# Layer 0 on a fixed SBUF map, layer 1's first loads issued inside layer 0, and its weights turned in six banks

## What is computed

```python
x = L0_attn_x                                  # [2, 1024, 512]
xn = _layernorm(x)
s = _L0_attn_ref(xn, Wq, bq, Wk, bk, Wv, bv)   # attention over the 16 dims of a head, per token
g = _silu(_L0_ffn_ref(xn, gate_w, ...))        # top 2 of 3 experts, chosen per batch entry
x = x + s * g
xn = _layernorm(x)
s = _L1_attn_ref(xn, Wq, Wk, Wv, Wo)           # causal attention with rotary positions, 32 heads, 8 key/value heads
g = _silu(_L1_ffn_ref(xn, qweight_gu, ...))    # gated FFN with 4-bit weights, unpacked in the kernel
x = x + s * g
```

## Time and profile before

| what | us |
|---|---|
| runs: median of three | 1476.67 |
| runs: lowest, highest | 1471.11, 1478.86 |
| the profiled execution's own time | 1469.95 |
| its span, from first to last instruction | 1468.2 |
| PE busy in the span | 1337.5 (91%) |
| DVE busy | 1058.9 (72%) |
| ACT busy | 618.0 (42%) |
| POOL busy | 334.9 (23%) |

### The profile page before, as it was taken

How to read it: one execution, slowest core, us unless ns; L and a number is a source line. 1 busy time by engine, 2 the same in 40 slices (tenths; PEclk the granted TensorE clock), 3 DMA queues, 4 the chain that set the end, 5 groups by cost and what they waited for, 6 DMA issues and landing times.

```text
span 1468.2 us, 19974 instructions
## 1 busy us (share of the span) xinstructions
PE 1337.5 (91%) x6642; PEld 924.9 (63%) x6642; DVE 1058.9 (72%) x2495; ACT 618.0 (42%) x859; POOL 334.9 (23%) x387
## 2 busy tenths in 40 slices
PE   3788988992998899999999998999999999999998
PEld 2557676772765677777777764555555555555467
DVE  6887978684787555555555476888888888888557
ACT  4633755452442111111111111666666666666662
POOL 2653667361332000000000000222112222212221
PEclk9978998995999899999999995999999999999999
DMA  6101200005344100000000050111122132231002
GB/s 213 63 24 63 72 16 29 0 29 184 96 124 135 53 27 27 25 22 22 22 13 12 5 97 0 34 34 34 34 44 56 34 90 62 63 68 29 2 29 86
DMA packets 45165, 76.11 MB, mean 52 GB/s; under 512 B 9556, under 2 KB 16804, under 8 KB 45076
## 3 DMA queue, kind: packets, MB, share of 16 engines
q1 hardware_dynamic: 43086, 73.36, 18.1%
q10 hardware_dynamic: 1990, 1.62, 0.4%
HBM read 55.67 MB, written 19.01 MB: 51 GB/s over the span
## 4 chain that ended last, share of the span: by engine, by line
PE 63%; DVE 6%; ACT 2%; issue 2%; DVEq 1%; ACTq 1%; DMA 0%; POOL 0%; SPq 0%; POOLq 0%
PE d_bank L1835 12%; PE d_bank L37 10%; PE d_bank L1875 10%; PE d_bank L1859 9%; PE d_bank L39 9%; PE d_bank L38 9%; PE d_bank L1883 1%; DVE mx_first L1595 1%; DVEq L1598 1%; DVE hl L1451 1%; DVE d_bank L1592 1%; PE d_bank L1704 1%; DVE hs L1448 1%; PE d_bank L1814 1%; ACT hh L1350 1%
## 5 line engine op out<-in xcount | busy, mean ns | idle before, releaser
L1386 ACT ACTIVATE prob<-d_bank 128x1024 f32<-128x1024 f32 (+3 forms) x384 | 302.3, 811 | 212.8 <-PE d_bank L1859 209.2
L1592 DVE CUSTOM_DVE_ANT_0 d_bank<-d_bank,mask 128x128 f32<-128x128 f32 (+3 forms) x512 | 246.2, 504 | 43.4 <-PE d_bank L1835 35.8
L1835 PE MATMUL d_bank<-kst,qst 96*128 96x512 f32 (+3 forms) x768 | 264.4, 386 | 5.4 <-DVE mx_first L1595 3.2
L1835 PEld LDWEIGHTS d_bank<-kst,qst 96*128 96x128 f32 x768 | 145.4, 194 | 145.1 <-DVE mx L1592 51.7
L1859 PE MATMUL d_bank<-qst,kst 98*128 98x512 f32 (+3 forms) x768 | 210.7, 357 | 0.5 <-ACT prob L1386 0.5
L1251 POOL TENSOR_SCALAR_AFFINE_SELECT prob<-prob 128x256 f32<-128x256 f32 x256 | 103.9, 406 | 449.9 <-ACT prob L1386 448.4
L1595 DVE TENSOR_REDUCE mx_first<-d_bank 128x1 f32<-128x512 f32 x256 | 176.3, 689 | 27.0 <-PE d_bank L1835 19.7
L1875 PE MATMUL d_bank<-prob,vst 128*32 128x512 f32 (+3 forms) x1536 | 164.5, 500 | 1.1 <-POOL prob L1251 1.1
L1342 ACT ACTIVATE hs<-d_bank 128x512 f32<-128x512 f32 (+1 forms) x44 | 26.3, 598 | 304.1 <-PE d_bank L39 304.1
L37 PE MATMUL d_bank<-xtl,wgh 128*128 (+1 forms) x352 | 141.3, 402 | 11.0 <-DVE v_all L1537 11.0
L1859 PEld LDWEIGHTS d_bank<-qst,kst 98*128 98x128 f32 x768 | 130.0, 192 | 19.0 <-ACT prob L1386 8.2
(11 more groups left out here) (256 smaller groups left out, 2419.1 us busy)
## 6 DMA issues: line engine op xcount, KB each, us to landing
wst<-L_ffn_w SPq DMA_DIRECT2D x8, 1024.0 KB, 6.9
qst<-q_scr SPq DMA_DIRECT2D x32, 256.0 KB, 4.8
qw<-L_ffn_qweight_gu SPq DMA_DIRECT2D x40, 128.0 KB, 2.6
xb<-L_attn_x SPq DMA_DIRECT2D x4, 1024.0 KB, 6.7
x_d<-xb SPq DMA_DIRECT2D x4, 1024.0 KB, 4.3
xb<-x_d SPq DMA_DIRECT2D x4, 1024.0 KB, 6.7
q_scr<-qh SPq DMA_DIRECT2D x16, 256.0 KB
q_scr<-ql SPq DMA_DIRECT2D x16, 256.0 KB
```

The source lines that it names most:

```text
L1386: act.activation(prob[:, c // 2 % 2, c % 2 * 2:c % 2 * 2 + 2, lo:], score_bank[c % 2][:, :, lo:], ACT.Exp, scale=D ** -0.5).then_inc(exp_d ...
L1592: dve.tensor_tensor_reduce(sc, sc, mask[:, CH - w:CH], 1.0, LEAST, ALU.add, ALU.max, mx[:, u, h % 2, h // 2, q:q + 1]).then_inc(spare_free, 1)
L1835: pe.matmul(spare_bank(number)[:, 0:w], qst[u][0:M_ROW, h // 2, q * P:q * P + P], kst[u][0:M_ROW, h % 2, at:at + w], start=True, stop=True ...
```

## The change

`layer0` gets a map of SBUF with fixed places; a class `Shared` holds what both layers use: the identity, the buffer of layer 1's tokens, the buffer of its weights, and three semaphores. The buffers' bytes overlap layer 0's staging buffers 0, 1 and 2, but no other tensor of layer 0. The last chunk's input and output (`xb[0]`) lie apart from all that layer 1 writes at first.

```diff
+class Shared:
+    def __init__(self, nc, ctx):
+        self.ident = place(nc, "ident", [P, P], F32, 203.5)
+        self.xb = place(nc, "xb1", [P, 2, TPC, E], F32, 0)
+        self.wqkv = place(nc, "wqkv", [P, QKT // P, E], F32, 123.5)
+        self.x1_stored, self.x_in, self.w_in = (ctx.enter_context(nc.semaphore("d_" + n)) for n in ("x1_stored", "xin0", "w_in"))
...
# layer0, SP: after the store of chunk c
+                if c == 2:
+                    sp.wait_ge(w1_ready, SL * B)
+                    sp.dma_start(shared.xb[:, 0], x1v[:, 0]).then_inc(shared.x_in, 16)
+                    sp.wait_ge(w2_ready, SL * B)
+                    Wq1, Wk1, Wv1 = next_qkv
+                    sp.dma_start(shared.wqkv[:, 0:KT], Wq1.rearrange("(o p) e -> p o e", p=P)).then_inc(shared.w_in, 16)
+                    sp.dma_start(shared.wqkv[:, KT], Wk1).then_inc(shared.w_in, 16)
+                    sp.dma_start(shared.wqkv[:, KT + 1], Wv1).then_inc(shared.w_in, 16)
-            sp.wait_ge(xout[0], 32)
             sp.wait_ge(xout[1], 16)
             sp.wait_ge(xout[2], 16)
...
# layer1, SP
-            sp.dma_start(xb[:, 0], x1v[:, 0]).then_inc(xin[0], 16)
-            sp.dma_start(wqkv[:, 0:KT], Wq.rearrange("(o p) e -> p o e", p=P)).then_inc(w_in, 16)
-            sp.dma_start(wqkv[:, KT], Wk).then_inc(w_in, 16)
-            sp.dma_start(wqkv[:, KT + 1], Wv).then_inc(w_in, 16)
             sp.dma_start(xb[:, 1], x1v[:, 1]).then_inc(xin[1], 16)
+            sp.dma_start(rotate[:, :], rotate_d).then_inc(rotate_in, 16)
+            sp.dma_start(cos[:, :], cos_d).then_inc(table_in, 16)
+            sp.dma_start(sin[:, :], sin_d).then_inc(table_in, 16)
+            small = lambda to, a: sp.dma_start(to, a).then_inc(s_in, 16)
+            small(sg[:, :], flat_gu(sc_gu, P))
...
             quants(0, 0, *PIECES[0])
             quants(0, 0, *PIECES[1])
+            sp.wait_ge(shared.x1_stored, 32)
             reload(2)
             keep_small_arrays()
+            sp.dma_start(mask[:, :], mask_d).then_inc(const_in, 16)
+            sp.dma_start(fixed[:, :, :], fixed_d).then_inc(const_in, 16)
...
# layer1, ACT: all fifteen loads leave its stream; the weights' parts come ahead of the tokens
-            normalize(0, range(TPC))
             for o in range(OT):
                 act.wait_ge(w_tp, o + 1)
-                act.activation(wth[:, :, o * P:o * P + P], bank[:, 2 + o % 2].rearrange("p (k q) -> p k q", k=KT),
+                act.activation(wth[:, :, o * P:o * P + P], bank[:, 2 + o].rearrange("p (k q) -> p k q", k=KT),
                                ACT.Copy).then_inc(w_hi, 1)
+            normalize(0, range(TPC))
             high_parts(0, range(TPC))
...
# layer1, PE
             pe.wait_ge(w_in, 48)
-            pe.wait_ge(ident_in, 16)
-            pe.wait_ge(const_in, 48)
             for o in range(OT):
-                if o >= 2:
-                    pe.wait_ge(w_lo, o - 1)
                 for k in range(KT):
-                    mm = pe.transpose(bank[:, 2 + o % 2, k * P:k * P + P], wqkv[:, o, k * P:k * P + P], ident[:, :])
+                    mm = pe.transpose(bank[:, 2 + o, k * P:k * P + P], wqkv[:, o, k * P:k * P + P], ident[:, :])
...
             turn_tokens(0, range(TPC))
             pe.wait_ge(w_lo, OT)
+            pe.wait_ge(rotate_in, 16)
```

More of the change, by code:

```diff
@@ L39, in three, with place, layer0 @@
     return pe.matmul(out, wh, mh, start=False, stop=last)
-def layer0(nc, x, Wq, bq, Wk, bk, Wv, bv, gate_w, gate_b, w1, b1, w2, b2, ident_d, strength_d, x1_d):
+def place(nc, name, shape, dt, at):
+    return nc.alloc_sbuf_tensor_at(name, shape, dt, offset=BASE + int(at * 1024))
+class Shared:
[4 more added lines that the diff above has]
+        self.x1_stored, self.x_in, self.w_in = (ctx.enter_context(nc.semaphore("d_" + n)) for n in ("x1_stored", "xin0", "w_in"))
+def layer0(nc, shared, x, Wq, bq, Wk, bk, Wv, bv, gate_w, gate_b, w1, b1, w2, b2, ident_d, strength_d, x1_d, next_qkv):
     with ExitStack() as ctx:
+        free = [[8, 123.5], [139.5, 171.5], [179.5, 203.5], [204, 207.75]]
         def sb(name, shape, dt=F32):
-            return ctx.enter_context(nc.sbuf_tensor(name, shape, dt))
+            size = math.ceil(math.prod(shape[1:]) / 8) / 32
+            room = next(r for r in free if r[1] - r[0] >= size)
+            room[0] += size
+            return place(nc, name, shape, dt, room[0] - size)
         def sem(name):
@@ L109, in layer0 @@
         x3_in = sem("x3_in")
-        xout = [sem(f"xout{u}") for u in range(UB)]
+        xout = [shared.x1_stored] + [sem(f"xout{u}") for u in range(1, UB)]
         w_in = [sem(f"w_in{u}") for u in range(WB)]
@@ L321, in high_part_w @@
                     act.wait_ge((f1_ps, f2_step)[n % 2], last)
[L322 removed]
+                act.activation((w1h, w2h)[n % 2][:, s], wst[n % WB][:, :, :], ACT.Copy).then_inc(hi_done, 1)
             def functions(c, m):
@@ new lines, in layer1 @@
+        cos, sin = place(nc, "cos", [P, T], F32, 16), place(nc, "sin", [P, T], F32, 20)
+        qf, qc = place(nc, "qf", [P, 2, CH], F32, 24), place(nc, "qc", [P, 2, CH], F32, 28)
+        wth, wtl = place(nc, "wth", [P, KT, QKT], F32R, 147.5), place(nc, "wtl", [P, KT, QKT], F32R, 159.5)
+        qh, ql = place(nc, "qh", [P, HALVES, CH], F32R, 189), place(nc, "ql", [P, HALVES, CH], F32R, 195)
+        rotate = place(nc, "rotate", [P, P], F32, 201)
+        stats, mv = place(nc, "stats1", [P, TPC, 6], F32, 201.5), place(nc, "mv1", [P, TPC, 2], F32, 201.625)
@@ L923, in layer1 @@
-        hot = place("hot", [2 * SD, 3, P], F32R, 187.5)
-        hs = place("hs", [P, 2, CH], F32, 189)
-        hh, hl = place("hh", [P, 2, CH], F32R, 193), place("hl", [P, 2, CH], F32R, 197)
-        ident, mask = place("ident", [P, P], F32, 203.5), place("mask", [P, CH], F32, 204)
-        mt = place("mt", [HG * QB, STACKS, P], F32R, 206)
-        fixed = place("fixed", [P, 2, 1], F32, 207.5)
-        qst = [place(f"qst{u}", [P, 2, T], F32R, at) for u, at in enumerate((112, 128, 171.5))]
-        kst = [place(f"kst{u}", [P, 2, T], F32R, at) for u, at in enumerate((120, 136, 179.5))]
@@ new lines, in layer1 @@
+        hh, hl = place(nc, "hh", [P, 2, CH], F32R, 193), place(nc, "hl", [P, 2, CH], F32R, 197)
+        mask = place(nc, "mask", [P, CH], F32, 204)
+        mt = place(nc, "mt", [HG * QB, STACKS, P], F32R, 206)
+        fixed = place(nc, "fixed", [P, 2, 1], F32, 207.5)
+        qst = [place(nc, f"qst{u}", [P, 2, T], F32R, at) for u, at in enumerate((112, 128, 171.5))]
+        kst = [place(nc, f"kst{u}", [P, 2, T], F32R, at) for u, at in enumerate((120, 136, 179.5))]
+        vst = place(nc, "vst", [P, STACKS, QB, 2 * D], F32, 144)
```

186 lines of the change are left out of this document (86 added, 100 removed).

## The result

The changed kernel took 1461.84 us (median of 10 runs, 1454.64 to 1464.27), the kernel before 1474.18 us in runs on the same chip (10 runs, 1469.97 to 1478.86). The ratio is 0.9906, its 95% interval 0.9884 to 0.9928: faster by 12.3 us, 0.9%. The forecast was 1460.5 in 1453 to 1472. The profiled execution of the changed kernel took 1457.57 us, with a span of 1455.8; the one of before had a span of 1468.2. That this agrees with the 12.3 us of the medians is luck: executions of one kernel lie up to 9 us apart. The median came 1.3 us above the forecast.

What follows compares the result with a forecast made beforehand. PE was taken to bound the kernel nearly everywhere. The seam's 15.4 us less 2.0 for the clock gave 13.4: 1456.6 for the profiled execution, 1460.5 from the median 1473.9, range 1453 to 1472.

Steps and rivals of the forecast that it cites:

- Prefetch in layer 0 costs nothing: Layer 0's last chunk: loading 1 MB of tokens and 1.5 MB of weights there costs compute nothing, with 25 us to spare.
- Handover, 3.95 us: Between the layers: without the wait for the last store, layer 1 starts at 342.85, 3.95 us less.
- Scale: Layer 1's start, DVE and POOL: the tokens' scale takes 5.2 us from the first statistic, ready at 348.1.
- Transposes, 5.9 us: Layer 1's start, PE: 24 weight transposes at the low clock take 5.9 us; with six banks none waits.
- Tokens: Layer 1's start: ACT normalizes in 2.93 us, then 4.16 us from first high part to first projection matmul, at 356.6.
- The seam, 15.4 us shorter: Passage between the layers: first projection matmul at 356.6 instead of 371.99, 15.4 us less, handover included.
- Rival 3: Seam: part was hidden anyway, small loads far late, or prefetch fails; gain 0 to 7 us, some 1470.5; chance 0.14.
- Small loads on SP, no cost: Layer 1's start: small loads issued by SP land between 2 us late and 7 us early; no cost taken.
- The clock, 2.0 us: PE after the seam: 1.7 us lost to one low stretch at the projections' start, 0.3 to slower token transposes.
- Rivals 1 and 4: PE's clock: early up and staying, gain 15.4, chance 0.2; or staying low in the projections, slower, chance 0.04.
- Layer 0's own end later than 342.1, which no step here allows.: End of layer 0: listed as a sign that the prediction is wrong, if its end came after 342.1.
- Removing one alone would give next to nothing.: Seam: tokens' scale, weights' landing and ACT's issuing were late together; removing only one gives next to nothing.

Runs made afterwards that it cites:

- e7: Changed kernel plus 33 transposes of the identity, output unread, in PE's pauses at layer 1's start; 1454.74 us, ratio 0.9871.
- e4: Changed kernel with layer 1's first tokens and weights loaded at layer 1's start again, not inside layer 0; 1469.03 us, ratio 0.9966.
- e6: Changed kernel with its moves undone except the prefetch of tokens and weights inside layer 0's last chunk; 1470.23 us, ratio 0.9977.
- e1: Changed kernel with layer 0's end waiting again for the last chunk's store to land; 1462.74 us, ratio 0.9923.
- e2: Changed kernel with the fourteen small loads back on ACT's queue, ahead of its first copies; 1465.59 us, ratio 0.9944.
- e5: Changed kernel with all moves undone, leaving only the fixed SBUF map and the identity loaded once; 1474.50 us, ratio 1.0008.

## Why the prediction was right, point by point

- **The bound.** PE nearly everywhere, and the seam the place of the gain: right. The time from the first projection matmul to the end moved by 2.24 us in all, and the low clock at the projections' start (2.6 by e7) accounts for it.
- **Prefetch in layer 0 costs nothing.** Right, shown by e4 and e6: the last chunk's length does not follow it.
- **Handover, 3.95 us.** Right: 3.83 by the profiles (4.73 less 0.90), 3.97 by e1. Layer 1's first instruction came at 0.90 us behind the store, where I had 0.77.
- **Scale.** 5.2 us from the first statistic to its end: measured 344.62 to 349.82, 5.20. The first statistic came 0.68 us after SP's first instruction, which I had at nothing.
- **Transposes, 5.9 us.** Mis-sized by 1.0: the run took 4.90. I had taken three groups of eight at 1.97 us; the chain gives 20 of them 4.48 us, 0.22 each, where 1.97 over eight is 0.25. The end of a pipelined run is in each group's time, and I counted it three times: some 0.4 us, an estimate from these rows. The other 0.6 fit the clock, which rose at 349 under the last transposes (0.97 in 349 to 350). Against this stands the 0.82 us from SP's first instruction to PE's first transpose, which I had at nothing. The two errors nearly cancel, so that ACT's last weight part ended 6.4 us after layer 1's start (350.35 less 343.94) where I had 6.55: that agreement is luck.
- **Tokens.** 2.93 us for the normalization and 4.16 from the first high part to the projections: measured 2.92, and 353.06 to 357.35, 4.29.
- **The seam, 15.4 us shorter.** Measured 15.60. Rival 3 falls: nothing was hidden.
- **Small loads on SP, no cost.** Right. The first small array (L1510) ran at 360.04, right behind DVE's statistics of the second chunk and with no wait named:

```profile
360.04 0.17 DVE L1510 CAST idf<-idx 128x4 f32<-128x4 int32 x1
```

  Sin landed 7.4 us after its issue at 346.52, some 12 us ahead of its first use at 366.5. The DMA engines were fully busy in 344 to 349, at 318 GB/s, as they had been before. What the move bought was ACT's time (e2). The Trainium skill, page "DMA: Bandwidth & Descriptors", section "Issuing engines are not separate DMA queues", says that SP's and ACT's transfers run on the same engines, so that another issuer saves only the sequencer's issue time; e2 agrees.
- **The clock, 2.0 us.** The right mechanism, a little short: 2.6 by e7. The stretch at the projections' start was 5.5 us (357.35 to 362.8), where I had taken 3.3 from the earlier trace rows. The 0.3 us for slower transposes of the tokens did not come: they took 1.35 and 1.22 us, at a clock of 1.00, where they had taken 1.43 and 1.23. Rivals 1 and 4 fall: the clock did not stay up, and it was up again by 363. The Trainium skill, page "TensorE: Matmul & The Clock Gate", section "Part 1: The HAM clock gate", says that activity is what lifts the throttle; e7, which adds activity and nothing else, agrees.
- **"Layer 0's own end later than 342.1, which no step here allows."** This is the step that failed, by 0.96 us. Its cause is not the change: layer 0's last store lay between 341.9 and 349.3 over the profiles in which layer 0's compute is untouched, at 343.04 and at 349.26 for one and the same kernel. I had treated as a fixed mark a time that moves with where the clock happens to be low.
- **"Removing one alone would give next to nothing."** Too strong: e6 gives 2.9 us of seam, most of it by the price of the issues of cos and sin.

What stays open is why the clock is low in one place in one execution and not in the next, and what the fills give in the median beyond 2.6 us. For the last chunk the profiles show one link. In before, e1, e5 and e6, and in no other, the clock was also low near 285 to 289. PE came later to its wait for ACT in these, but left it at the same time, 12.3 us after the third store; so the wait was shorter (2.2 to 2.9 us, not 3.8 to 3.9), and the low stretch behind it was short or missing. That this is the cause was not tested. One larger stretch was left alone by the change and by every fill, the passage from the FFN to the attention; filling it was not tried. In the changed kernel:

```profile
871.00:906.00 35.00, 28.96 (x77) 17.70 (x79) 24.04 (x71) 4.48 (x6) 2.40 (x6) 0.51 0.00 0
```

## What to carry to other kernels

Where several things are late together at a seam, price the whole path to the next bound and not its parts: here the parts, undone one by one, cost 25 us of the seam, and all together 16. After such a repair, look at what the busiest engine now does in its short pauses, since its clock may take back a part of the gain; here work that nobody reads, put into them, held it up. And before a mark in a trace is called fixed, see two executions of the same kernel.

## What the runs showed of the hardware

- **The clock of one and the same code differs between executions.** In 171 to 185 us one execution of the changed kernel ran at 1.00, another at 0.51. The chunk that holds this stretch took 4.0 us more; with the two chunks behind it, layer 0's end moved by 6.2 us and the span by 6.4. The runs of this kernel lie 9 us apart, so such differences could make most of their scatter.
- **A fallen clock can stay low under full load for long.** In 243 to 254 and in 315 to 326 of the changed kernel PE was busy for all 11 us, and the clock was 0.53 and 0.54. At the projections' start the same took some 6 us.
- **It fell in a row of short pauses.** At the seam PE's idle times were 1.4, 2.1 and 1.6 us with some 1.3 us of work between them, and the clock fell; with transposes in them (e7: 0.35, 0.63 and 0.37 us idle) it did not.
- **The issue of a DMA was cheaper with less in flight.** The issues of cos and sin took 4.4 and 4.6 us together on ACT's queue with all first loads of the layer beside them (before, e5), 2.1 with 2.5 MB less (e2, e6), and 1.3 on SP's queue in the changed kernel. With the 2.5 MB in SP's own queue (e4) they took 1.2, but two smaller loads there took 1.87 and 2.30.
